# Reordering the last two iterations of a fused cross-attention, linear-recurrence and feed-forward kernel

## The reference

```
x = x + softmax(LN(x) Wq (ctx Wk)^T / 8) (ctx Wv) Wo + bo          8 heads of 64
x = x + recurrence(LN(x) ln_g + ln_b) Wo2                          4 heads of 64
    w = sigmoid(xn Wx Ww + bw), k = xn Wk, v = xn Wv, r = sigmoid(xn Wr)
    state = (1 - w) * state + k v^T ;  out = r . state              over 32 steps
x = x + gelu(LN(x) U1 V1 + b1) U2 V2 + b2                          256 -> 64 -> 1024 -> 64 -> 256
```

## Time and profile before

| | |
|---|---|
| median of 3 runs | 1008.64 us |
| the three runs | 1011.24, 1008.64, 1008.29 us |
| the profiled execution | 1010.61 us |
| its span, first to last instruction | 1008.6 us |
| TensorE, matmuls | 980.3 us busy, 97% |
| TensorE, weight loads (beside the matmuls) | 788.6 us, 78% |
| ScalarE, VectorE, GpSimd | 532.0, 506.4, 187.0 us |
| mean granted TensorE clock | 0.994 |

### The profile page before, as it was taken

How to read it: one execution, slowest core, us unless ns; L and a number is a source line. 1 busy time by engine, 2 the same in 40 slices (tenths; PEclk the granted TensorE clock), 3 DMA queues, 4 the chain that set the end, 5 groups by cost and what they waited for, 6 DMA issues and landing times.

```text
span 1008.6 us, 21326 instructions
## 1 busy us (share of the span) xinstructions
PE 980.3 (97%) x8328; PEld 788.6 (78%) x8328; DVE 506.4 (50%) x1189; ACT 532.0 (53%) x1343; POOL 187.0 (19%) x324
## 2 busy tenths in 40 slices
PE   4989999999999999999999999999999999999997
PEld 3667888787887878788787878888787878877875
DVE  4543655454555545455554644555354554536352
ACT  3445446465564556556365655646555564654431
POOL 0010303031130312103030220303112030302130
PEclk9999999999999999999999999999999999999999
DMA  7322222213222222222222223222222312122000
GB/s 280 116 87 85 86 70 73 87 47 96 77 86 77 75 73 62 86 87 87 76 76 67 67 78 95 72 91 62 76 72 78 96 57 94 43 73 84 12 1 21
DMA packets 58001, 78.89 MB, mean 78 GB/s; under 512 B 10288, under 2 KB 39856, under 8 KB 57904
## 3 DMA queue, kind: packets, MB, share of 16 engines
q1 hardware_dynamic: 56192, 76.38, 24.4%
q10 hardware_dynamic: 1712, 1.16, 0.4%
HBM read 73.05 MB, written 4.46 MB: 77 GB/s over the span
## 4 chain that ended last, share of the span: by engine, by line
PE 92%; DVE 2%; ACT 2%; SPq 2%; DMA 1%; issue 1%; POOL 0%; DVEq 0%; POOLq 0%
PE gb L331 19%; PE scores L388 11%; PE scores L391 8%; PE acc L417 7%; PE acc L413 7%; PE gb L450 6%; PE gb L511 6%; PE ptp L400 5%; PE acc L418 5%; PE gb L560 3%; PE gb L550 3%; PE gb L363 3%; PE gb L340 2%; SPq L274 2%; PE gb L525 2%; PE gb L567 2%
## 5 line engine op out<-in xcount | busy, mean ns | idle before, releaser
L625 ACT ACTIVATE probs<-scores,nmax 128x257 f32<-128x257 f32 x256 | 119.1, 472 | 204.7 <-DVE nmax L766 204.7
L766 DVE TENSOR_REDUCE nmax<-scores 128x2 f32<-128x514 f32 x128 | 88.7, 693 | 223.1 <-PE scores L391 223.1
L972 POOL TENSOR_TENSOR ptm<-probs,head 128x32 f32<-128x32 f32 x128 | 35.0, 273 | 623.5 <-DVE probs L773 623.5
L388 PE MATMUL scores<-raw_t,qk 128*128 128x257 f32 x512 | 133.4, 384 | 2.2 <-ACT qk L665 1.3
L388 PEld LDWEIGHTS scores<-raw_t,qk 128*128 128x128 f32 x512 | 88.0, 192 | 9.9 <-issue 1.7
L773 DVE TENSOR_TENSOR probs<-probs,rinv 128x514 f32<-128x514 f32 x128 | 89.0, 695 | 4.4
L391 PE MATMUL scores<-raw_t,qk 64*128 64x257 f32 x512 | 90.3, 430 | 0.0
L417 PE MATMUL acc<-pt,raw_n 128*128 128x256 f32 x256 | 89.6, 432 | 0.0
L400 PE MATMUL ptp<-ident,probs 128*128 128x128 f32 x512 | 78.2, 276 | 8.0 <-DVE probs L773 7.8
L413 PEld LDWEIGHTS acc<-pt,raw_n 128*64 128x64 f32 x1024 | 55.4, 136 | 36.2 <-issue 33.4
L630 ACT ACTIVATE pt<-ptp 128x512 f32<-128x512 f32 x128 | 77.0, 602 | 11.2 <-PE ptp L400 11.0
(11 more groups left out here) (145 smaller groups left out, 2252.3 us busy)
## 6 DMA issues: line engine op xcount, KB each, us to landing
raw_t<-in_ctx_t SPq DMA_DIRECT2D x128, 258.0 KB, 3.0
raw_n<-in_ctx_n SPq DMA_DIRECT2D x128, 192.0 KB, 2.4
xb<-in_x SPq DMA_DIRECT2D x16, 256.0 KB, 2.7
vsp<-tail_values SPq DMA_DIRECT2D x256, 2.0 KB
out<-ob SPq DMA_DIRECT2D x16, 256.0 KB, 2.2
xin<-in_x SPq DMA_DIRECT2D x15, 256.0 KB, 2.8
khat<-in_wq ACTq DMA_DIRECT2D x1, 512.0 KB, 4.2
wv<-in_wv SPq DMA_DIRECT2D x1, 512.0 KB, 6.2
```

What stands on the lines that cost most here:

```text
L388: mm(scores[:, r, 0:L], w[:, b, r * P:(r + 1) * P], x[:, 0, 0:L], start=True, stop=False)
L625: go(probs[n % 2][:, r, 0:L], scores[:, r, 0:L], ACT.Exp, bias=nmax[:, r:r + 1], accum_out=rsum[:, r:r + 1]).then_inc(s["exp_ready"], 1)
L766: v_.tensor_reduce(nmax[:], scores[:, :, 0:L], AX.X, ALU.max, negate=True)\
```

## The change

Five things are changed. In ENDING, Qf and Y3 of group 13 go from before Y1 of group 15 to behind Y2 of group 14 and to before z; Qf and Y3 of group 14 go from before Sp and before O2 of group 15 to behind O2 and behind Y2, so that Sp of 15 follows H2 of 14. The counts in BUSY are new. Qf waits for H1 before its first four products and for H3 before its last four, in every iteration. ScalarE does one gelu on two numbers in iteration 17, slot 2. On VectorE Y3 has its place in slot 3 instead of slot 1 from iteration 16 on, and Y1 waits itself for ob_ready.

```
 NEXT, OLD, OLDER = NG - 1, NG - 2, NG - 3
-ENDING = {(NG, 0): [("Sq", OLD), ("WV", NEXT), ("Qf", OLDER)], (NG, 1): [("O2", OLD), ("Y3", OLDER), ("Y1", NEXT)],
-          (NG, 2): [("Y2", OLD), ("XT2", NEXT)], (NG, 3): [("z", NEXT)], (NG, 4): [("k", NEXT), ("XT3", OLD)],
-          (NG, 5): [("r", NEXT), ("Pf", OLD)], (NG, 6): [("v", NEXT), ("H0", OLD)],
-          (NG, 7): [("H2", OLD), ("Qf", OLD), ("Sp", NEXT)],
-          (NG + 1, 0): [("Sq", NEXT), ("Y3", OLD), ("O2", NEXT)], (NG + 1, 2): [("Y2", NEXT)],
-          (NG + 1, 3): [("XT3", NEXT)], (NG + 1, 4): [("Pf", NEXT)], (NG + 1, 5): [("H0", NEXT)],
-          (NG + 1, 7): [("H2", NEXT), ("Qf", NEXT), ("Y3", NEXT)]}
+ENDING = {(NG, 0): [("Sq", OLD), ("WV", NEXT)], (NG, 1): [("O2", OLD), ("Y1", NEXT)],
+          (NG, 2): [("Y2", OLD), ("Qf", OLDER), ("XT2", NEXT)], (NG, 3): [("Y3", OLDER), ("z", NEXT)],
+          (NG, 4): [("k", NEXT), ("XT3", OLD)], (NG, 5): [("r", NEXT), ("Pf", OLD)],
+          (NG, 6): [("v", NEXT), ("H0", OLD)], (NG, 7): [("H2", OLD), ("Sp", NEXT)],
+          (NG + 1, 0): [("Sq", NEXT), ("O2", NEXT)], (NG + 1, 1): [("Qf", OLD), ("Y2", NEXT)],
+          (NG + 1, 2): [("Y3", OLD)], (NG + 1, 3): [("XT3", NEXT)], (NG + 1, 4): [("Pf", NEXT)],
+          (NG + 1, 5): [("H0", NEXT)], (NG + 1, 7): [("H2", NEXT), ("Qf", NEXT), ("Y3", NEXT)]}
...
-BUSY = {("Y2", OLD): 4, ("XT2", NEXT): 5, ("H2", OLD): 2, ("Y3", OLD): 1, ("O2", NEXT): 3, ("Y2", NEXT): 9,
-        ("XT3", NEXT): 1, ("Pf", NEXT): 1, ("H2", NEXT): 3, ("Qf", NEXT): 1}
+BUSY = {("Qf", OLDER): 5, ("Y3", OLDER): 8, ("H2", OLD): 2, ("O2", NEXT): 1, ("Y3", OLD): 15,
+        ("XT3", NEXT): 3, ("Pf", NEXT): 2, ("H2", NEXT): 1, ("Qf", NEXT): 2}
...
             def qf_(g):
                 out_ = tile("Qf", g)
-                drained("H3", g)
                 for c in range(8):
+                    if c % 4 == 0:
+                        drained(f"H{c // 2 + 1}", g)
                     r0 = 64 * (c % 2)
                     last = mm(out_[r0:r0 + 64, 0], u2[:, c], hid[:, c], start=c < 2, stop=c > 5)
...
+                    if (i, b) == (NG + 1, 2):
+
+                        go(warm[:], half[:], ACT.Gelu_apprx_tanh)
...
                 elif n == "Y1":
                     dve.wait_ge(s["xb_ready"], g + 1)
+                    if g > 1:
+                        dve.wait_ge(s["ob_ready"], g - 1)
...
+            AT_END = [list(x) for x in GAPS]
+            AT_END[1] = [[], [], ["O2-2", "Y1-1"]]
+            AT_END[3] = GAPS[3][:2] + [["Y3-3"]]
+
             def gap(i, b, k):
-                for item in GAPS[b][k]:
+                for item in (AT_END if i >= NG else GAPS)[b][k]:
```

## The result

The changed kernel takes 1014.29 us (median of 6 executions, 1013.88 to 1017.36), the kernel before 1009.42 (6, 1007.85 to 1011.24). The ratio is 1.0054, 95% interval 1.0037 to 1.0071: 5.4 us slower by the ratio, 4.9 by the medians. 1012.7 was predicted, as 2.1 more than the profiled execution's 1010.61. The direction and the steps held.

A forecast was written before the change was run, and what follows sets the result against it. TensorE was taken as the bound, 92% of the span. At full clock the sum was -0.7 us (-3.0 at Y2, +2.57 before XT3); +2.8 for a clock fall made +2.1 on 1010.61, so 1012.7, range 1009.2 to 1014.8.

The forecast's parts named there:

- Fillers past their gates: Last iterations: each filler costs 0.43 us; XT2 starts 1.4 us behind its gate, XT3 2.57 late.
- The rival that fillers cost half: Every filler reaching past a gate costs 0.22 us, so the kernel gets faster, 1003.1 to 1006.0; chance 0.13.
- The forecast of +2.4 between executions without a fall: Whole kernel: fillers make the change 2.4 us slower against an execution without a clock fall, 1011.0 from 1008.64.
- Moving Qf13 and Y3 of 13: Iteration 16: only O2 stays between WV and Y1, so Y1 starts at 952.10, 1.57 us earlier.
- Moving Qf14: Ahead of S: the wait for the gelus goes, rhat is late next; 1.95 us idle, S at 976.84 against 977.06.
- The fall of the clock: In S: clock falls again, at 979.8 for 6.8 us, with less work around the same products; +2.8 us taken.
- the rival without a fall: S stretch: the clock does not fall, giving 1009.9, or 1011.0 against a run that had none; chance 0.22.
- the gap behind S: Between S and O2: TensorE stands still 0.93 us for VectorE's four copies, counted among reasons for a fall.
- the -3.0 at Y2: Y2 at full clock starts at 984.83 instead of 987.87; 3.1 us of the old time is the low clock.
- The gelu for the table: ScalarE, iteration 17: the added gelu loads no table and runs in idle time; 0 either way.
- The split wait: Qf in the 13 attention iterations: taken as 0, at the other end 2.0 us; as a rival 1014.7, chance 0.05.
- The last stretch: XT3 to the end: gelus 0.5 us later, 0.74 gained by half of Qf, sum -0.24 against 11.79.

The follow-up runs named there:

- trim: Changed kernel with six filler counts cut to what the gates leave, 19 fillers fewer: 1008.17 us, ratio 0.9986 to the kernel before.
- only15: Changed kernel with one number changed, 7 fillers instead of 15 behind Y3 of group 14: 1010.61 us, ratio 1.0007 to the kernel before.
- after_gaps: Changed kernel, long counts kept, with 6 fillers instead of 2 behind H2 of 14 and 2 behind Sq of 15: 1013.67 us, ratio 1.0035.
- part1: Kernel before with only Qf and Y3 of group 13 moved, 1 and 4 fillers there: 1007.30 us, ratio 0.9977.
- qf_back: trim with Qf of group 14 back ahead of S, 2 fillers behind Sq and 3 behind O2: 1003.53 us, ratio 0.9936 to the kernel before.
- trim_h2_6: trim with 6 fillers instead of 2 behind H2 of group 14, ahead of S: 1006.00 us, ratio 0.9961 to the kernel before.
- trim_sp3: trim with 3 fillers added between the two halves of S of group 15: 1009.86 us, ratio 0.9998 to the kernel before.
- no_fill: Changed kernel with all fillers taken out: 1008.30 us, ratio 0.9993 to the kernel before.
- before_split: Kernel before with only the split wait in Qf, in all iterations: 1008.62 us, ratio 0.9989.
- trim_h6_sq2: trim with 6 fillers ahead of S and 2 behind Sq: 1003.97 us, ratio 0.9945 to the kernel before.

## Why the prediction was right or wrong

The steps, with 1.2 us taken off the positions of after:

| | predicted | measured |
|---|---|---|
| Y1 starts | 952.10 | 952.1 |
| XT2 | 960.25 | 960.7 |
| S starts, wait ahead of it | 976.84, 1.95 | 977.2, 1.74 |
| clock falls, for | 979.8, 6.8 | 979.8, 6.8 |
| O2 | 982.2 | 982.7 |
| Y2 | 987.6 | 988.0 |
| XT3 (Y2 + 8.89) | 996.5 | 996.9 |
| last add ends | 1008.1 | 1008.5 |

- **Fillers past their gates: right.** 0.43 each; XT2 1.7 us and XT3 3.5 us behind gates that VectorE had opened. trim and only15 give the time back. The rival that fillers cost half is out. The forecast of +2.4 between executions without a fall was a little low: the three of after_gaps at 0.998 are 3.1 us over the kernel before at 0.998 on that chip (1011.3 and 1008.2).
- **Moving Qf13 and Y3 of 13: right.** Y1 starts at o_l's gate, 1.6 earlier; 5 and 8 fillers ate it; in part1's trace it is whole, 1.55 us at the start of S.
- **Moving Qf14: right.** rhat took the place of the gelus as what is late. qf_back shows that the move is worth nothing by itself, and trim_h2_6 that the idle time it left ahead of S had a cost.
- **The fall of the clock: right that it comes, in place and length; half right on why.** "Less work around the same products, so I take a fall again" held, 6 executions of 6 at 0.995 or less. The fall in the profile of before, which the forecast leans on, stands in the earlier trace rows: the clock goes from 1.00 to 0.50 at about 979.9, 2.9 us behind the start of S at 977.06, and is back at about 986.8. TensorE had not stood still in S; ahead of it came Qf14, and ahead of Qf14 a wait of 1.27 us. In the experiments' expectations I went further and gave it to the S products alone, and trim_sp3 and trim_h2_6 refuted that. The traces show falls behind both a long wait and none: in no_fill the clock fell 0.4 us behind the 2.8 us gap ahead of XT3, in the changed kernel 2.6 us into S behind a wait of only 1.74 us, and in after_gaps 3.0 us into S without a pause around it. So the rival without a fall was wrong here. The prediction counted the gap behind S (0.93, measured 0.85) as a reason for the fall; it is not what begins it. In the changed kernel the clock fell at 981.0 and that gap came at about 983.1, and in each of the nine traces with a fall in the S stretch it began 2.3 to 3.6 us behind S's start, before any gap behind S; the bounds that I took, 1.5 and 4.8 us, were my estimate and wider than that. The other length, half of 6.8, is in the profile of before near its start (3.4 us from 24.2 on) and at the end of before_split; that dense work behind the fall is what halves it was my estimate too, and no run shows it: in the profiles of before and before_split the same steps follow S, and the fall took 6.8 and 3.4 us.
- **The failed step: what the sum was set against.** I credited the change with the whole old fall ("the -3.0 at Y2 (3.1 of it the old fall)"), because the profiled execution of before had one, and wrote that timed runs without it would pull "my range up, not the value". Of the 76 executions of the kernel before that were timed beside the experiments, 37 were at 0.998 and took 1007.7 to 1009.6, mean 1008.6. 12 at 0.997 took 1.8 us more on average, 27 at 0.995 and less 2.8 more (1010.3 to 1013.0). So half of the executions pay nothing, and the average one pays 1.3 us; the changed kernel always pays. With 1.3 credited instead of 3.1, the prediction's own terms give +2.4 + 2.8 - 1.3 = +3.9 in place of +2.1; measured are 4.9 by the medians and 5.4 by the ratio, whose interval, 3.7 to 7.2 us, holds 3.9.
- **What remains.** Between the two profiled executions, both with a full fall, the end is 2.5 us longer (last table load to the end of the span, 69.3 before and 71.8 after) where 2.1 was forecast; from XT2 on the steps are 0.3 to 0.5 later than forecast. Two of the six executions of the changed kernel had a lower clock than the others (0.992 and 0.993: 1017.36 and 1015.36), and they raise the ratio more than the median.
- **The small parts.** The gelu for the table: nothing, right. The split wait: nothing in the attention iterations was nearly right, 0.3 us as far as two traces tell. The last stretch: forecast 11.55 from XT3 to the end, measured 11.6.

Not settled: why one execution falls and another does not. The share at 0.995 or less goes from 27 in 76 before, 1 in 12 in part1 (same steps around S) and 5 in 10 in after_gaps to 6 in 6 in the changed kernel with the same products, and nothing that was varied here brings it to zero surely. Nor is it settled what the pause behind S does. Filling it too took the clock from 0.997 in 6 of 9 executions (trim_h2_6) to 0.998 in 5 of 6 (trim_h6_sq2), on another chip and with no trace of a 0.997 execution of the first.

## What to carry to other kernels

Before summing a change against a profile, ask whether the profiled execution is the usual one: an event that costs up to 3 us and comes in half of the executions belongs into the base with its frequency. The mean granted clock of each timed run is what shows it. Filler work is priced like any other: count it up to the input's arrival and no further (0.43 us for each one past it here), but do put it where the trace shows TensorE standing still ahead of light work in which its clock fell; here 19 fillers fewer in some places and 6 more in two others were 10 us together.

## What the hardware showed unexpectedly

- Light products behind a short wait: 1.74 to 1.78 us of standing still and then 64x128 by 32-column products went with a fall in every execution of the changed, the trimmed and the only15 kernel (29 of 29 at 0.995 or less; in their traces the clock fell 2.6 to 3.2 us into the products). The same products without that wait ahead did so in 3 of 9 (trim_h2_6), 5 of 10 (after_gaps), 1 of 6 (trim_h6_sq2) and 0 of 5 (qf_back).
- Falls at the end had three lengths in these traces: 3.4 us (before_split), 6.8 us (the kernel before and six others) and 10.2 us (trim_sp3).
- xn of Y2, 0.73 us in the changed kernel, took 1.71 us in part1, where GpSimd's 128x512 add ran beside it (and 1.68 in the kernel before, at 992.36). part1, which keeps that order, on VectorE:

```profile
988.89 1.71 DVE L760 TENSOR_SCALAR xn<-x,mv,rstd 128x256 f32<-128x256 f32 x2 [0.81 <-POOL rstd L1042]
```

and on GpSimd:

```profile
988.83 1.30 POOL L1038 TENSOR_TENSOR ob<-x,b 128x512 f32<-128x512 f32 x1
```
